# Four more shared tiles held on chip instead of added row by row

## The reference

```
x = x + attention(layernorm(x), ctx)
y = layernorm(x)
routed[token] += weight * (silu(y Wg_e) * (y Wu_e)) Wd_e   # for each of the token's 6 experts e; 128 places per expert
shared = (silu(y Sg) * (y Su)) Sd
out = x + routed + shared
```

## Time and profile before

| what | value |
|---|---|
| device time, median of 3 runs | 813.7 us (813.09 to 814.16) |
| the profiled execution's own time | 814.21 us |
| its span | 812.4 us |
| TensorE busy | 765.2 us, 94% |
| VectorE busy | 591.4 us, 73% |
| ScalarE busy | 452.0 us, 56% |
| GpSimd busy | 321.2 us, 40% |
| DMA | 180.34 MB, mean 222 GB/s |

### The profile page before, as it was taken

How to read it: one execution, slowest core, us unless ns; L and a number is a source line. 1 busy time by engine, 2 the same in 40 slices (tenths; PEclk the granted TensorE clock), 3 DMA queues, 4 the chain that set the end, 5 groups by cost and what they waited for, 6 DMA issues and landing times.

```text
span 812.4 us, 10918 instructions
## 1 busy us (share of the span) xinstructions
PE 765.2 (94%) x3886; PEld 649.0 (80%) x3886; DVE 591.4 (73%) x1172; ACT 452.0 (56%) x797; POOL 321.2 (40%) x258
## 2 busy tenths in 40 slices
PE   6999999999999999999998999999999989987983
PEld 5888887888788887888777888888878878877772
DVE  6437486775767756765577899999988989987821
ACT  3424323333334323343173898999988889986720
POOL 1001010346104451055304456666666666665533
PEclk9999999999999999999999999999999999999997
DMA  4961345321533216403455999999999999999878
GB/s 165 333 223 53 103 175 188 105 87 70 211 153 105 104 66 247 155 1 118 170 223 168 303 346 345 338 358 343 352 348 350 346 336 356 345 331 356 200 140 163
DMA packets 58996, 180.34 MB, mean 222 GB/s; under 512 B 7664, under 2 KB 8048, under 8 KB 54512
## 3 DMA queue, kind: packets, MB, share of 16 engines
q1 hardware_dynamic: 39312, 137.64, 45.1%
q0 software_dynamic: 19632, 42.02, 22.8%
HBM read 143.33 MB, written 43.92 MB: 230 GB/s over the span
## 4 chain that ended last, share of the span: by engine, by line
PE 46%; DMA 18%; DVE 11%; POOL 10%; issue 8%; ACT 5%; SPq 1%; POOLq 0%; DVEq 0%; ACTq 0%
PE bank L1097 8%; PE bank L1098 8%; PE bank L1099 8%; DMA out_rows<-eo,idx_all 5%; POOL xg L1327 4%; DMA stage<-wvT_in 3%; DMA out_rows<-product,idx_all 3%; POOL out_rows L1335 3%; POOL second_sum L1335 3%; PE scores L1097 3%; PE scores L1099 3%; PE scores L1098 3%; PE bank L905 3%; DMA second_sum<-eo,idx_all 2%; DMA second_sum<-product,idx_all 2%
## 5 line engine op out<-in xcount | busy, mean ns | idle before, releaser
L421 POOL DMA_INDIRECT table<-rows,slot x72 | 80.4, 1117 | 157.7 <-DVEq L832 114.0
L1460 DVE TENSOR_TENSOR gu_lo<-raw,gu_hi 128x768 fp32r<-128x768 f32 x128 | 122.1, 955 | 24.5 <-ACT gu_hi L1380 23.2
L1380 ACT ACTIVATE gu_hi<-raw 128x768 fp32r<-128x768 f32 x128 | 107.2, 840 | 12.0 <-DMA raw<-expert_in 11.9
L1327 POOL DMA_INDIRECT xg<-x_rows,idx_all x64 | 75.6, 1181 | 58.6 <-DVEq L668 26.8
L1097 PE MATMUL ps_gu<-gu_hi,xgT_hi 128*128 128x384 f32 x256 | 92.0, 359 | 2.6 <-DVE xgT_lo L1460 2.6
L1099 PE MATMUL ps_gu<-gu_hi,xgT_lo 128*128 128x384 f32 x256 | 86.7, 339 | 0.0
L1098 PE MATMUL ps_gu<-gu_lo,xgT_hi 128*128 128x384 f32 x256 | 86.6, 338 | 0.0
L449 ACT ACTIVATE qT<-bank 128x512 fp32r<-128x512 f32 x32 | 19.2, 599 | 114.8 <-PE bank L1099 109.2
L454 ACT ACTIVATE pbuf<-scores,negmax 128x1024 f32<-128x1024 f32 x16 | 17.9, 1117 | 70.2 <-DVE negmax L603 70.2
L581 DVE TENSOR_TENSOR qT<-bank,qT 128x512 fp32r<-128x512 f32 x32 | 22.0, 689 | 47.2 <-ACT qT L449 47.2
L1097 PEld LDWEIGHTS ps_gu<-gu_hi,xgT_hi 128*128 128x128 f32 x256 | 48.6, 190 | 3.0 <-DVE xgT_lo L1460 3.0
(11 more groups left out here) (276 smaller groups left out, 2233.8 us busy)
## 6 DMA issues: line engine op xcount, KB each, us to landing
raw<-expert_in SPq DMA_DIRECT2D x64, 1024.0 KB, 12.2
rest<-rest_in SPq DMA_DIRECT2D x32, 256.0 KB, 8.6
x_rows<-pbuf SPq DMA_DIRECT2D x17, 256.0 KB, 2.1
stage<-wkT_in SPq DMA_DIRECT2D x4, 1024.0 KB, 4.8
stage<-ctxT_in SPq DMA_DIRECT2D x4, 1024.0 KB, 4.8
stage<-wvT_in SPq DMA_DIRECT2D x4, 1024.0 KB, 9.0
stage<-ctx_in SPq DMA_DIRECT2D x4, 1024.0 KB, 9.4
stage<-woT_in SPq DMA_DIRECT2D x4, 1024.0 KB, 4.8
```

The source lines that it names most:

```text
L421: pool.indirect_dma_start(out=table, out_offset=bass.IndirectOffsetOnAxis(ap=slot[:, i, k:k + 1], axis=0), in_=rows[:, i, k, :], in_offset ...
L1327: pool.indirect_dma_start(out=xg[:, e % 3, :], out_offset=None, in_=x2_rows, in_offset=index(("expert", e))).then_inc(gathered[e % 3], 16)
L1380: act.activation(gu[n % GU_SLOTS][0][part], gate_up_of(n, part), ACT.Copy).then_inc(weights_high, 1)
L1460: return dve.tensor_tensor(lo, x, hi.bitcast(F32), ALU.subtract)
```

## The change

A further batch, batch 1 (`HELD`), is taken out of the chains. ScalarE still evicts its four tiles, each to a buffer of its own, and waits for no add; no add follows. The chains then have 72 sets, and their turns and buffers go by a new number `c` without these four. In the closing time GpSimd loads the rows of two batches of the second table, 1 MB each, and merges two batches instead of three. VectorE adds each held tile to its loaded rows before it takes the first tile of batch 2, and GpSimd adds the four sums to the output, ahead of the four of batch 2.

```diff
-CHAINED = len(SETS)
+HELD = LAST - 1
+CHAIN_NO = {what: c for c, what in enumerate(what for what in SETS
+                                             if what[0] == "expert" or what[1][0] != HELD)}
...
-    sb("above_raw2", [P, D])
+    held = [sb("held0", [P, D])[:, :]]
...
+    held.append(products[0])
...
-    second_rows = raw[0][:, :].rearrange("p (i d) -> p i d", d=D)
+    second_rows = {b: raw[n][:, :].rearrange("p (i d) -> p i d", d=D) for n, b in enumerate((HELD, LAST))}
...
         def add_rows(what):
-            r = SET_NO[what]
-            if r >= 2:
-                pool.wait_ge(added[r % 2], r // 2 * 16)
-            pool.wait_ge(eo_ready, r + 1)
-            pool.indirect_dma_start(out=(t["out"], second_sum)[r % 2], out_offset=index(what),
-                                    in_=eo[r % EO], in_offset=None,
-                                    compute_op=ALU.add).then_inc(added[r % 2], 16)
+            if what not in CHAIN_NO:
+                return
+            c = CHAIN_NO[what]
+            if c >= 2:
+                pool.wait_ge(added[c % 2], c // 2 * 16)
+            pool.wait_ge(eo_ready, SET_NO[what] + 1)
+            pool.indirect_dma_start(out=(t["out"], second_sum)[c % 2], out_offset=index(what),
+                                    in_=eo[c % EO], in_offset=None,
+                                    compute_op=ALU.add).then_inc(added[c % 2], 16)
...
-            pool.wait_ge(added[n], CHAINED // 2 * 16)
+            pool.wait_ge(added[n], len(CHAIN_NO) // 2 * 16)
         pool.wait_ge(weights_split, len(PIECES))
-        pool.dma_start(second_rows, second_sum[LAST * S:(LAST + 1) * S, :].rearrange("(i p) d -> p i d", p=P)
-                       ).then_inc(second_loaded, 16)
-        merge(0, LAST).then_inc(summed, 16)
+        for b in (HELD, LAST):
+            pool.dma_start(second_rows[b], second_sum[b * S:(b + 1) * S, :].rearrange("(i p) d -> p i d", p=P)
+                           ).then_inc(second_loaded, 16)
+        merge(0, HELD).then_inc(summed, 16)
         merge(LAST + 1, B).then_inc(summed, 16)
+        for n, tile in enumerate(TILES_OF[HELD]):
+            pool.wait_ge(held_added, n + 1)
+            pool.indirect_dma_start(out=t["out"], out_offset=index(("shared", tile)), in_=held[tile[1]],
+                                    in_offset=None, compute_op=ALU.add).then_inc(summed, 16)
...
         def out_rows(what):
             r = SET_NO[what]
             act.wait_ge(dn_full, r + 1)
-            if r >= EO:
-                act.wait_ge(added[r % 2], (r // 2 - 1) * 16)
+            if what not in CHAIN_NO:
+                act.activation(held[what[1][1]], ps_dn[:, r % 2, :], ACT.Copy).then_inc(eo_ready, 1)
+                return
+            c = CHAIN_NO[what]
+            if c >= EO:
+                act.wait_ge(added[c % 2], (c // 2 - 1) * 16)
...
                 r = SET_NO["shared", n]
+                if n[1] == 0:
+                    dve.wait_ge(second_loaded, 32)
+                    for i in range(NT):
+                        dve.tensor_tensor(held[i], held[i], second_rows[HELD][:, i, :],
+                                          ALU.add).then_inc(held_added, 1)
                 dve.wait_ge(dn_full, r + 1)
-                dve.wait_ge(second_loaded, 16)
```

More of the change, by code:

```diff
@@ L1160 @@
         SETS.append(("shared", EVENT_AT[_e][1]))
-CHAINED = len(SETS)
+HELD = LAST - 1
+CHAIN_NO = {what: c for c, what in enumerate(what for what in SETS
+                                             if what[0] == "expert" or what[1][0] != HELD)}
+assert len(CHAIN_NO) % 2 == 0
 SETS += [("shared", tile) for tile in TILES_OF[LAST]]
@@ L1188, in experts @@
     raw.append(sb("raw2", [P, ROW]))
-    sb("above_raw2", [P, D])
+    held = [sb("held0", [P, D])[:, :]]
     gu_hi1 = sb("gu_hi1", [P, GU], F32R)
-    sb("above_gu_hi1", [P, D])
+    held.append(sb("held1", [P, D])[:, :])
     ssilu, shid, products = [], [], []
@@ L1197, in experts @@
     raw.append(sb("raw3", [P, ROW]))
-    sb("above_raw3", [P, D])
+    held.append(sb("held2", [P, D])[:, :])
     dn_lo2 = sb("dn_lo2", [P, D], F32R)
@@ L1248, in experts @@
     second_loaded = sem("second_loaded")
+    held_added = sem("held_added")
     tile_added = sem("tile_added")
@@ L1372, in gpsimd @@
                                     in_offset=None, compute_op=ALU.add).then_inc(summed, 16)
-        pool.wait_ge(summed, 32 + 16 * NT)
+        pool.wait_ge(summed, 32 + 32 * NT)
     def act_weights(act, first, past):
@@ L1412, in out_rows @@
             act.wait_ge(dn_full, r + 1)
-            if r >= EO:
-                act.wait_ge(added[r % 2], (r // 2 - 1) * 16)
+            if what not in CHAIN_NO:
[4 more added lines that the diff above has]
+                act.wait_ge(added[c % 2], (c // 2 - 1) * 16)
             scale = tab[:, what[1], 1:2] if what[0] == "expert" else 1.0
-            act.activation(eo[r % EO], ps_dn[:, r % 2, :], ACT.Copy, scale=scale).then_inc(eo_ready, 1)
+            act.activation(eo[c % EO], ps_dn[:, r % 2, :], ACT.Copy, scale=scale).then_inc(eo_ready, 1)
         act_silu(act, 3)
@@ L1520, in step @@
                 r = SET_NO["shared", n]
+                if n[1] == 0:
[3 more added lines that the diff above has]
+                                          ALU.add).then_inc(held_added, 1)
                 dve.wait_ge(dn_full, r + 1)
-                dve.wait_ge(second_loaded, 16)
-                dve.tensor_tensor(eo[r % EO], ps_dn[:, r % 2, :], second_rows[:, n[1], :],
+                dve.tensor_tensor(eo[r % EO], ps_dn[:, r % 2, :], second_rows[LAST][:, n[1], :],
                                   ALU.add).then_inc(tile_added, 1)
```

## The result

The changed kernel takes 816.8 us, the kernel before 812.0 (medians of 20 runs each; the 813.7 of the first three runs lay high). The ratio of the two is 1.0048, with a 95% interval from 1.0034 to 1.0062: 3.9 us slower, where 1.7 us faster was forecast. In a later comparison it was 1.0060 (1.0035 to 1.0084). The profiled execution of the change took 819.81 us with a span of 818.1, 5.7 us over the span before, so it shows somewhat more than the usual loss.

A forecast was written before the change was run, and what follows sets the result against it. The prediction took the stage to run at the limit of its DMA engines. A stage gain of 3.6 us less 1.9 us of longer closing time made 1.7 us less: 812.0 us from 813.7, range 806.5 to 815.5.

The forecast's parts named there:

- What bounds the stage: Expert stage: DMA engines full, expert 59's weights 0.2 us from binding; a new ScalarE wait for them near 735 to 742.
- The stage's gain, g = 1.5 + 2.1: Expert stage: g, the time by which the last weights' split and all after it come earlier, taken as 3.6 us.
- The first term: Up to 743: two adds fewer bring expert 59's weights sooner, half of 2.6 us plus 0.2 of slack, 1.5 us.
- the wait for an add ended at the same time: At expert 59's split, 743.45: why no wait for its weights was booked, although they landed with only 0.2 us of slack.
- The prediction's own argument: Stage up to 743: the chains catch up on experts' adds, so nearly as many run and weights come hardly sooner.
- The lower bound of g, 0: Expert stage: no gain, if expert 59's weights land when they did and something else takes the rest.
- The second term: Expert stage after 743: the 2.1 us wait at 755.99 goes too, as the chains have caught up.
- The closing time, +1.9: After the stage: the closing time grows by 1.9 us, between 1.0 and 5.5.
- The DMA engines' sum: Closing time: loads +2.6 us, merges -5.2, adds +5.2, so 2.6 us longer; 1.9 taken since part falls into gaps.
- T + 22.4: Closing time: GpSimd issues the last of eight adds 22.4 us after the closing time begins, where it was 16.9.
- The closing time outweighs the stage: Rival, chance 0.17: eight adds queue on GpSimd and land as late as now, +5.5 us against 3.6 gained; 815.6 us.
- Nothing but the slack: Rival, chance 0.20: expert 59's weights land as before, TensorE loses half of the 2.1; gain 1.3 us, 814.3, no change.

The follow-up runs named there:

- closing time alone: All 76 sets go through the chains as in the kernel before, with the change's closing time; 3.7 us slower than the kernel before.
- eight buffers: The kernel before with eight buffers instead of four for evicted sets, all adds and the old closing time kept; 1.1 us slower than before (-0.4 to +2.5).
- the stage alone: The changed kernel with the old closing time put back and batch 1's shared part left out of the result; 2.4 us slower than the kernel before.
- the direct adds: The changed kernel with the four held sums added by plain instead of indirect accumulating DMAs; 3.8 us slower than the kernel before.
- the change again: The changed kernel, unaltered, timed and profiled a second time; 4.9 us slower than the kernel before.
- batch 2 later: The changed kernel with batch 2's first product begun at step 62 instead of 60; 3.4 us slower than the kernel before.
- the change without the 2 MB: The changed kernel without loading batch 2's 2 MB of activations, using batch 3's instead; 6.3 us faster than the kernel before.
- the one with them last and batch 2 later: The changed kernel with batch 2's 2 MB of activations loaded behind the last weights and batch 2 begun at step 62; 5.9 us faster than the kernel before.

## Why the prediction was wrong

*What bounds the stage: right.* Full DMA engines, 59's weights with 0.2 us of slack, and the wait for them that takes the adds' place were all in the text, and the wait came (7.5 us, forecast "near 735 to 742", there until 746.8).

*The stage's gain, g = 1.5 + 2.1: this is the step that failed.* It had the last split 3.6 us earlier; it came 1.6 us later (767.74 against 765.06, less the 1.1 us of later start). The first term, "I take half of the two adds' 2.6 us, 1.3, with 0.2 of slack", took the landing of 59 from one execution, where the split follows the issue of the 2 MB by 17.5 us, and let it come sooner. In the other kernels with the 2 MB at that place it was 20.7 (closing time alone), 21.3 (eight buffers) and 20.8 to 22.4 (four tiles out).

Behind the 0.2 of slack stands a misreading: "the wait for an add ended at the same time". In the profile before it ended 4.6 us earlier:

```profile
738.84 0.69 ACT L1416 ACTIVATE eo<-ps_dn,tab 128x512 f32<-128x512 f32 x1 [4.19 <-DMA out_rows<-eo,idx_all]
```

ScalarE then worked without a break until it took 59's weights at 743.45. The wait for the add had pushed this work back to where the weights had just landed, and so hid them. In the change ScalarE was through with it at 739.3 and stood until 746.78. With the stage of before in the closing-time-alone kernel the add's wait of 3.4 us did not hide them whole, and 2.3 us showed. How it is in most executions of the kernel before is not known, as only one was profiled.

Nor did leaving the adds out bring the weights sooner. From the eviction near 624 to the split of 59 it is 119.4 and 120.4 us with the stage of before, and 120.6 to 121.7 in the five profiles with the tiles out and the 2 MB at that place. The prediction's own argument, that other adds would run instead, was right, and it still took 1.3 us for their relief: up to the landing GpSimd issued 28 adds and 22 gathers from there before, 27 and 24 in the change. That the gathers, freed from the adds ahead of them, took the place is read from these counts; no run held them back. The lower bound of g, 0, excluded a loss, and the stage alone lost 2.4 us.

The second term, 2.1 from the wait at 755.99, came as 0.8. The wait did go. What took its place, by the profiles, is the longer pause: TensorE stood 7.2 us at one time, where before the longest of its four waits was 4.3. It then ran some 5 us at the lower clock, before some 3. In a stretch of 2 us it did 8 matmuls at the lower clock and 11 to 15 at the higher; by this the longer time at the lower clock costs some 0.7 of the missing 1.3 us (an estimate). The load for expert 63, asked for later (752.19, before 750.26), shows no cost: no wait stands before its split at 767.74. The rest stays open.

*The closing time, +1.9: right in its mechanism, too small.* It is 3.1 us longer (32.3 to 32.7 in the kernels that have it, against 29.3 to 29.4), inside the 1.0 to 5.5 given. The DMA engines' sum had said 2.6; taking 0.7 off it for gaps was the error, and 0.5 over the sum stays open. The issue of the last add was forecast for T + 22.4 and came at T + 22.9, but the direct adds show that this did not matter.

*The rivals.* "The closing time outweighs the stage" was the one on the right side, but not by its own mechanism: it had g = 3.6 and +5.5. "Nothing but the slack" was nearest in kind (a longer pause of TensorE that takes the later gain) and gave 814.3. No rival joined a stage without gain to the closing time's cost, which is what happened: of the 3.9 us about 0.8 for the stage and 3.1 for the closing time.

## What to carry to other kernels

Before pricing the removal of a wait, list what else is due soon after it, and how its due time varies over executions: a transfer that lands while the engine works off what the booked wait had held back has no wait of its own in the profile and is the next bound. Where the DMA engines are full, a few MB that nobody waits for have a price, and what else is waited for at their place decides it: the same 2 MB at the same place cost 1.9 us in one kernel and 10.2 in the other. In the changed kernel it was 7.3 us with them last, and nothing that can be told from zero with batch 2 begun later as well. Two changes that each gain nothing (held tiles, activations last) gained 5.9 us with a third, because each uncovered the next wait at one place; so test them together before dropping one.

## What the runs showed that was not expected

- A plain load of 1 MB behind others in the stage issued from 680 to 698, took 11 to 13 us in the profile before and some 14 to 17 in those of the stage alone and of the closing time alone, where the three programs do the same. Landing times counted from the issue differ by some 3 us between executions here, so a slack read from one profile is no better than that.
- TensorE's granted clock fell with each long pause: from 740 to 750 it was 0.51 (the change again, ScalarE's wait 8.5 us), 0.66 (batch 2 later, 9.0) and 0.70 (the change, 7.5). From 730 to 760 it stayed at 1.00 in the change without the 2 MB and in the one with them last and batch 2 later, where ScalarE's waits for DMAs were under 1 us.
- An accumulating DMA of 128 rows issued directly takes less time of GpSimd than an indirect one (four in some 3.5 us against four in some 7.4), and lands no sooner when the engines are full.
